# A decoder layer on one core: row maxima from 32-row score chunks, normalisations on ScalarE, softplus steps regrouped, and three of every eight C products on VectorE

## The chip, the cores and the metric

One core of one Trainium2 chip runs the whole program. The metric is the device time of one execution in microseconds, the median of several runs. The kernel before took 5991.21 us (median of 3 runs, 5989.22 to 5993.96).

## The reference

The layer works on x of 64 batches x 128 tokens x 512 features, fp32, with a context of the same shape. Three residual parts follow each other, each on a layer norm of x:

```
x = x + mixer(layernorm(x))              # selective scan
x = x + cross_attention(layernorm(x), ctx)
x = x + experts(layernorm(x))            # top 2 of 8
```

The mixer projects 512 to 2 x 1024 channels (h and gate), runs a causal convolution of 4 taps and silu on h (giving u), projects u to a step size (through 128) and to B and C of 16 states, and takes `dt = softplus(...)`, `dA = exp(dt * A)`, `dBx = dt * u * B`. The state `h[t] = dA[t] * h[t-1] + dBx[t]` runs over the 128 tokens for each of 1024 channels x 16 states; `y = sum over states of h * C + D * u`, times silu(gate), projected back to 512.

The attention treats the 512 features as positions: 8 heads of 16, and each position attends to those at most 64 away (`|q - k| <= 64`), softmax over the keys. The output goes through a projection, relu, a product with ctx and a last projection. The experts part is a router over 8 experts with the top two kept, and experts of width 16.

## The kernel before, in words

The work goes in groups of two batches (GB = 2), 32 groups. One round of the main loop carries three groups at once: group g in the scan of the mixer, group g+1 in the mixer's front (norm, input projections, convolution, B and C, step sizes), group g-1 in the attention, and group g-2 in the experts. Each engine has its own instruction list for a round (the function `iteration` of each engine's block). These lists are written out by hand, step by step; every engine works strictly in its order, and semaphores say when a step may start. The loop body holds two rounds.

The scan is 64 steps s per round: 8 channel blocks ic of 128 (s // 8) x 8 pairs r of states (s % 8), two states and two batches in one tile of 128 x 512. A step passes through all engines:

- ScalarE, `decays` (L479): two exponentials of 128 x 254 into PSUM bank s % 2 (DAR = 2), so it waits for the scan of step s-2.
- GpSimd, `times_b` (L296): du x B into slot s % 8 of the ring (RING = 8), when TensorE has finished with step s-8.
- VectorE, `scan` (L1417): the recurrence, from PSUM and the ring slot, into the ring slot.
- GpSimd or VectorE, `times_c` (L305 or L1402): the slot times C. VectorE does those in `DVE_C`, before: s % 8 = 7.
- TensorE, `y_sum` (L1018, L1025): transposes two steps at a time and sums them over states in PSUM, and frees the slots. The order of y_sum is fixed, a pair waits for both products.

Around it, per round:

- Layer norms, six per round (three uses "a", "t", "e", for mixer, attention and experts, x 2 batches). VectorE takes the statistics and adds epsilon (`norm_stats`, L1363 to L1372), GpSimd takes the power -0.5 (`rstd`, L284), VectorE subtracts the mean and multiplies (`normalise`, L1376, 128 x 512). TensorE then transposes (L896) or projects (L919) the result.
- Softplus, four pairs q of channel blocks: ScalarE makes z, abs, exp(-|z|) in `soft` (two buffers), 1 + exp in `tmp` (L507), ln (L511) in place; VectorE corrects the rounding in `soft_step` 1 to 3 and makes dt x u in step 4 (L1386 to L1397). The ln waits for step 1, since it overwrites `soft`.
- Attention, per batch (i): four blocks of 128 query rows. In the score block `s` (L942) TensorE first writes a mask with `masked` (L906: band values through an identity in bf16, 16 matmuls, the first of them 32x128 and the others 32x32), adds the scores of 8 heads (a 32-row group for each of four heads, keys in a window of 192 or 256), and VectorE takes the negated row maximum (L1464) from all four banks. The next score block waits for this maximum. The maxima are transposed (L952) and added to the queries (L1471) so that a second, transposed set of scores `st` (L906, L969) gives exponentials (L591) without a further subtraction.
- ScalarE's functions lie in table sets; exp, ln and silu are in three, and an ACT_TABLE_LOAD stands where the set changes.
- SP's queue brings the input projection in pieces, x, the context, and after the last use of a C row pair r (step 56 + r) the next round's B and C rows (`spread`, waiting for hcd_done or hcp_done by which engine makes that product).

## Time and profile before

| | |
|---|---|
| median of the runs | 5991.21 us |
| profiled execution | 5965.38 us |
| its span | 5963.5 us |
| busy in the span | GpSimd 5176.7, TensorE 5036.6, VectorE 4912.6, ScalarE 4024.9 us |
| mean granted clock of TensorE | 0.951 of full speed |

Busy time is the union of an engine's instructions; instructions of VectorE and ScalarE overlap a little at their ends. The profile names engines PE (TensorE), DVE (VectorE), ACT (ScalarE), POOL (GpSimd). A round of the loop repeats 32 times with a shorter first and last part, so a stretch of the middle shows the kernel better than the whole span.

### The profile page before, as it was taken

To read this page: it belongs to the slowest core of one execution; us is meant where nothing else is said; L and a number is where in the kernel's file an instruction comes from. 1 tells how busy PE (TensorE), PEld (TensorE's weight loads), DVE (VectorE), ACT (ScalarE), POOL (GpSimd) and SP (SyncE) were. 2 spreads that over 40 slices of the span, in tenths; PEclk is the share of its full clock that TensorE was granted. 3 is DMA by queue.
4 is the path that set the end of the run, shared out by engine and by line. 5 is a ranking of instruction groups with operands and counts; after the bars stand their busy time and mean duration, and the time that the engine had idled before them with its cause. 6 is when DMAs were issued, how large, how long until landed. Compare 5 with 4: busy or idle time off the path is not lost.

```text
span 5963.5 us, 117386 instructions
## 1 busy us (share of the span) xinstructions
PE 5036.6 (84%) x40772; PEld 3515.4 (59%) x40772; DVE 4912.6 (82%) x6563; ACT 4024.9 (67%) x7680; POOL 5176.7 (87%) x4040
## 2 busy tenths in 40 slices
PE   5788888888888888888888888888888888888876
PEld 3556666666565666556566666666656566566643
DVE  3788988888888888988888888888888888888862
ACT  3676776777676777777677666767667677676651
POOL 3998999899999989999899899989999899898870
PEclk8899999999999999999999999999999999999985
DMA  3221211121211221211121111221112121111100
GB/s 103 66 65 31 72 60 65 65 68 35 68 65 60 68 68 35 65 65 63 65 68 55 45 65 64 68 65 49 50 65 67 61 68 48 52 65 63 54 11 6
DMA packets 114455, 348.74 MB, mean 58 GB/s; under 512 B 12912, under 2 KB 14704, under 8 KB 113776
## 3 DMA queue, kind: packets, MB, share of 16 engines
q1 hardware_dynamic: 113904, 341.48, 17.6%
q8 instruction: 336, 5.51, 0.4%
q14 instruction: 215, 1.76, 0.1%
HBM read 323.60 MB, written 17.83 MB: 57 GB/s over the span
## 4 chain that ended last, share of the span: by engine, by line
PE 33%; issue 21%; DVE 19%; ACT 13%; POOL 13%; DVEq 1%; ACTq 0%; POOLq 0%; DMA 0%; SPq 0%
DVE ring L1417 8%; POOL ring L296 7%; PE ps L1073 6%; POOL ring L305 5%; ACT ps L479 5%; PE ps L906 4%; PE ps L1025 4%; PE ps L942 3%; PE ps L969 3%; PE ps L1093 2%; DVE nmax L1464 2%; ACT probs_mem L591 2%; PE ps L1102 2%; PE ps L1108 2%; PE ps L1005 2%
## 5 line engine op out<-in xcount | busy, mean ns | idle before, releaser
L296 POOL TENSOR_TENSOR ring<-du,bc 128x512 f32<-128x512 f32 x2048 | 2747.9, 1355 | 291.4 <-PE ps L1025 182.8
L1417 DVE TENSOR_TENSOR_SCAN ring<-ps,ring 128x512 f32<-128x512 f32 x2048 | 2459.4, 1211 | 455.2 <-ACT ps L479 431.8
L305 POOL TENSOR_TENSOR ring<-ring,bc 128x512 f32<-128x512 f32 x1792 | 2389.4, 1342 | 300.9 <-DVE ring L1417 287.9
L479 ACT ACTIVATE ps<-delta,a_neg 128x254 f32<-128x254 f32 x4096 | 1770.0, 468 | 525.0 <-DVE ring L1417 519.1
L1025 PE MATMUL ps<-ident,ring 128*128 128x128 f32 x8192 | 1127.5, 284 | 83.4 <-POOL ring L305 74.3
L1025 PEld LDWEIGHTS ps<-ident,ring 128*128 128x128 f32 x8192 | 972.0, 146 | 275.1 <-issue 186.4
L906 PE MATMUL ps<-band,ident_bf 32*32 32x512 bf16 (+1 forms) x8192 | 402.5, 406 | 320.8 <-DVE nmax L1464 88.5
L1464 DVE TENSOR_REDUCE nmax<-ps 128x8 f32<-128x1536 f32 (+1 forms) x256 | 516.9, 2019 | 168.0 <-PE ps L942 166.2
L591 ACT ACTIVATE probs_mem<-ps 128x768 f32<-128x768 f32 (+1 forms) x512 | 445.4, 909 | 212.6 <-PE ps L969 208.4
L1073 PE MATMUL ps<-xt_a,w_in 128*128 128x256 f32 x2048 | 483.7, 390 | 55.9 <-ACT gate_t L550 50.0
L1093 PE MATMUL ps<-w_in,xt_a 128*128 128x256 f32 x2048 | 502.7, 401 | 15.5 <-DVE hc L1557 8.1
L1073 PEld LDWEIGHTS ps<-xt_a,w_in 128*128 128x128 f32 x2048 | 384.1, 192 | 158.4 <-ACT gate_t L550 76.3
L1055 PE MATMUL ps<-w_outp,yz 128*128 128x512 f32 x1024 | 469.7, 602 | 0.0
L1093 PEld LDWEIGHTS ps<-w_in,xt_a 128*128 128x128 f32 x2048 | 403.4, 201 | 109.3 <-issue 34.9
L906 PEld LDWEIGHTS ps<-band,ident_bf 32*32 32x32 bf16 (+1 forms) x8192 | 115.9, 89 | 581.7 <-issue 199.6
L1557 DVE SCALAR_TENSOR_TENSOR hc<-ps,conv_w,hc 128x254 f32<-128x254 f32 (+2 forms) x768 | 363.4, 474 | 61.3 <-ACT hc L536 39.5
L980 PE MATMUL ps<-probs_mem,v_aug 128*32 128x192 f32 (+1 forms) x4096 | 239.4, 365 | 102.2 <-ACT probs_mem L591 102.2
L1402 DVE TENSOR_TENSOR ring<-ring,bc 128x512 f32<-128x512 f32 x256 | 312.4, 1220 | 2.3
L1055 PEld LDWEIGHTS ps<-w_outp,yz 128*128 128x128 f32 x1024 | 191.4, 194 | 192.2 <-issue 190.0
L942 PE MATMUL ps<-qk 32*128 32x192 f32 (+1 forms) x4096 | 303.3, 416 | 0.0
L969 PE MATMUL ps<-qk 32*128 32x192 f32 (+1 forms) x4096 | 279.9, 389 | 0.0
L919 PE MATMUL ps<-xb,w_qk 128*128 128x512 f32 x512 | 245.4, 602 | 36.1 <-DVE x_res L1435 35.7
(129 smaller groups left out, 6575.2 us busy)
## 6 DMA issues: line engine op xcount, KB each, us to landing
w_in<-in_w_in SPq DMA_DIRECT2D x256, 512.0 KB, 3.7
bc<-bc_rows SPq DMA_DIRECT2D x256, 512.0 KB, 4.3
x_new<-in_x SPq DMA_DIRECT2D x32, 512.0 KB, 6.9
x_res<-in_x SPq DMA_DIRECT2D x32, 512.0 KB, 6.1
enc<-in_ctx SPq DMA_DIRECT2D x64, 256.0 KB, 4.4
out<-x_att SPq DMA_DIRECT2D x32, 512.0 KB, 2.9
w_outp<-in_w_outp SPq DMA_DIRECT2D x1, 2048.0 KB, 8.1
bc_rows<-bc_sb SPq DMA_DIRECT2D x32, 32.0 KB, 1.5
```

Of the source, the lines that this page charges most:

```text
L296: nc.gpsimd.tensor_tensor(ring[:, s % RING, :].rearrange("p (n t) -> p n t", n=2), du[:, q % 2, (ic % 2) * NT:(ic % 2 + 1) * NT].rearrange ...
L305: nc.gpsimd.tensor_tensor(ring[:, s % RING, :], ring[:, s % RING, :], bc[:, s % RS, 2:4, :].rearrange("p a t -> p (a t)"), ALU.mult).then_ ...
L479: nc.scalar.activation(ps[:, s % DAR, (n % 2) * NT:(n % 2 + 1) * NT].rearrange("p (b t) -> p b t", b=GB)[:, :, 1:T], delta[:, ic, :].rearr ...
L591: nc.scalar.activation(probs[:, :, blk, lo:hi], ps[:, PS_ATT:PS_ATT + 4, (n % 2) * WIN + lo:(n % 2) * WIN + hi], ACT.Exp).then_inc(p_done, 1)
L906: nc.tensor.matmul(ps[rows, PS_ATT + hp, :].rearrange("p (j w) -> p j w", j=2), ident_bf[r:r + 32, cols], band[r:r + 32, a:a + 1, :].to_br ...
L942: last = nc.tensor.matmul(ps[:, PS_ATT + hp, j * WIN + lo:j * WIN + hi], qk[r:r + 32, j, n * P:(n + 1) * P], qk[r:r + 32, 2 + j, at:at + h ...
L1025: last = nc.tensor.matmul(ps[:, PS_Y, b * T:(b + 1) * T], ring[:, t % RING, n * NT + b * T:n * NT + (b + 1) * T], ident[:], start=False, s ...
L1055: last = nc.tensor.matmul(ps[:, PS_ATT + b, :], yz[:, ic, b * T:(b + 1) * T], w_outp[:, ic, :], start=(ic == 0), stop=(ic == NI - 1))
L1073: last = nc.tensor.matmul(ps[:, PS_B, a * NT:(a + 1) * NT], w_in[:, slot, k, a * P:(a + 1) * P], xt_a[:, k, :], start=(k == 0), stop=(k == ...
L1093: last = nc.tensor.matmul(ps[:, PS_B, b * NT:(b + 1) * NT], xt_a[:, k, b * T:(b + 1) * T], w_in[:, slot, k, :], start=(k == 0), stop=(k == ...
L1417: nc.vector.tensor_tensor_scan(ring[:, s % RING, :], ps[:, s % DAR, :], ring[:, s % RING, :], 0.0, ALU.mult, ALU.add).then_inc(h_done, 1)
L1464: nc.vector.tensor_reduce(nmax[:, n].rearrange("p j (a r) -> p a j r", r=32)[:, :, :, DH], ps[:, PS_ATT:PS_ATT + 4, :].rearrange("p a (j w ...
```

## The change

- `DVE_C` becomes s % 8 in (1, 4, 7): VectorE makes 24 of 64 C products of a round, GpSimd 40.
- The layer norms' last step goes to ScalarE as `Identity(scale * x + bias)`. VectorE makes the bias, -mean x rstd, in a new op of one column (`shift`); `rstd` takes both batches in one call for "e" and "a". The step that was on VectorE is gone.
- The scores for the row maxima are made in chunks of 32 query rows: a chunk sees 160 keys (NEAR = 128 + 32) and no more, so a block holds 2 x 160 columns in each bank. The mask of such a chunk is the same for each of the four (`near`, four 32x128 matmuls with a new constant `ident4`, and eight short ones more in the first and last block). The scores are 32 matmuls of 32x32 where 8 of 32x128 were. The row maximum reads 1280 elements a row.
- `masked`, now for the transposed scores alone, has 16 matmuls of 32x32, without the wide first one; a semaphore that nobody waits for is raised ahead of it.
- Softplus: `soft` has one buffer, the ln writes a tile of its own (`lnv`) and waits for the exp alone; abs and exp of the next pair wait for the correction step and the ln of the one before.
- The lists of all four engines are written anew (only the number and kind of steps told above differ).

```diff
+    NEAR = P + 32
-    DVE_C = [s for s in range(64) if s % 8 in (7,)]
+    DVE_C = [s for s in range(64) if s % 8 in (1, 4, 7)]
...
-        soft = sb("soft", [P, 2, 2 * NT])
+        soft = sb("soft", [P, 2 * NT])
+        lnv = sb("lnv", [P, 2 * NT])
...
+        ln_nm = {k: sb("ln_nm_" + k, [P, GB]) for k in "ate"}
...
# GpSimd
-            def rstd(use, g, b):
-                pool.wait_ge(ln_eps[use], g * GB + b + 1)
-                nc.gpsimd.tensor_tensor(ln_rs[use][:, b:b + 1], ln_rs[use][:, b:b + 1], neg_half[:, 0:1],
-                                        ALU.pow).then_inc(ln_rstd[use], 1)
+            def rstd(use, g, b, n=1):
+                pool.wait_ge(ln_eps[use], g * GB + b + n)
+                nc.gpsimd.tensor_tensor(ln_rs[use][:, b:b + n], ln_rs[use][:, b:b + n], neg_half[:, 0:n],
+                                        ALU.pow).then_inc(ln_rstd[use], n)
...
# ScalarE
+            def normalise(use, g, b, dst, src, done):
+                act.wait_ge(ln_shift[use], g * GB + b + 1)
+                nc.scalar.activation(dst, src[:, b, :], ACT.Identity, scale=ln_rs[use][:, b:b + 1],
+                                     bias=ln_nm[use][:, b:b + 1]).then_inc(done, 1)
...
             def soft_exp(g, q):
                 pq = g * NQ + q
-                reached(act, dt_done, pq - 1)
+                reached(act, sp_c, pq)
+                reached(act, sp_ln, pq)
...
             def soft_ln(g, q):
-                act.wait_ge(sp_c, g * NQ + q + 1)
-                nc.scalar.activation(soft[:, q % 2, :], soft[:, q % 2, :], ACT.Ln, bias=1.0).then_inc(sp_ln, 1)
+                pq = g * NQ + q
+                act.wait_ge(sp_exp, pq + 1)
+                reached(act, dt_done, pq)
+                nc.scalar.activation(lnv[:], soft[:], ACT.Ln, bias=1.0).then_inc(sp_ln, 1)
...
# TensorE
+            def near(n):
+                for hp in range(4):
+                    r = 32 * hp
+                    nc.tensor.matmul(ps[:, PS_ATT + hp, 0:NJ * NEAR].rearrange("p (j w) -> p j w", j=NJ),
+                                     ident4[r:r + 32, :], band[r:r + 32, 0:1, 0:NEAR].to_broadcast([32, NJ, NEAR]),
+                                     start=True, stop=False, skip_group_check=True)
+                for a, lo, hi in {0: ((0, 0, 64), (1, 0, 32)), NBLK - 1: ((2, P, NEAR), (3, P - 32, NEAR))}.get(n, ()):
+                    for hp in range(4):
+                        r = 32 * hp
+                        nc.tensor.matmul(ps[32 * a:32 * a + 32, PS_ATT + hp, 0:NJ * NEAR].rearrange("p (j w) -> p j w", j=NJ)[:, :, lo:hi],
+                                         ident_bf[r:r + 32, r:r + 32], band[r:r + 32, 3:4, 0:hi - lo].to_broadcast([32, NJ, hi - lo]),
+                                         start=False, stop=False, skip_group_check=True)
...
             def masked():
                 for a in range(4):
                     for hp in range(4):
                         r = 32 * hp
-                        wide = a == 0 and hp == 0
-                        rows, cols = (slice(0, P), slice(0, P)) if wide else (slice(32 * a, 32 * a + 32), slice(r, r + 32))
-                        nc.tensor.matmul(ps[rows, PS_ATT + hp, :].rearrange("p (j w) -> p j w", j=2),
-                                         ident_bf[r:r + 32, cols], band[r:r + 32, a:a + 1, :].to_broadcast([32, 2, WIN]),
-                                         start=(a == 0 or hp > 0), stop=False, skip_group_check=True)
+                        nc.tensor.matmul(ps[32 * a:32 * a + 32, PS_ATT + hp, :].rearrange("p (j w) -> p j w", j=2),
+                                         ident_bf[r:r + 32, r:r + 32], band[r:r + 32, a:a + 1, :].to_broadcast([32, 2, WIN]),
+                                         start=True, stop=False, skip_group_check=True)
...
-                    masked()
+                    near(n)
                     for j in range(NJ):
-                        for hp in range(4):
-                            r = 32 * hp
-                            last = nc.tensor.matmul(
-                                ps[:, PS_ATT + hp, j * WIN + lo:j * WIN + hi],
-                                qk[r:r + 32, j, n * P:(n + 1) * P], qk[r:r + 32, 2 + j, at:at + hi - lo],
-                                start=False, stop=True, skip_group_check=True)
+                        for a in range(4):
+                            k0 = n * P + 32 * a - 64
+                            lo, hi = max(0, -k0), min(NEAR, H - k0)
+                            for hp in range(4):
+                                r = 32 * hp
+                                last = nc.tensor.matmul(
+                                    ps[32 * a:32 * a + 32, PS_ATT + hp, j * NEAR + lo:j * NEAR + hi],
+                                    qk[r:r + 32, j, n * P + 32 * a:n * P + 32 * a + 32], qk[r:r + 32, 2 + j, k0 + lo:k0 + hi],
+                                    start=False, stop=True, skip_group_check=True)
...
# VectorE
-            def normalise(use, g, b, dst, src, done):
+            def shift(use, g, b):
                 dve.wait_ge(ln_rstd[use], g * GB + b + 1)
-                nc.vector.tensor_scalar(dst, src[:, b, :], ln_mv[use][:, b, 0:1], ln_rs[use][:, b:b + 1],
-                                        ALU.subtract, ALU.mult).then_inc(done, 1)
+                nc.vector.tensor_scalar(ln_nm[use][:, b:b + 1], ln_mv[use][:, b, 0:1], ln_rs[use][:, b:b + 1], -1.0,
+                                        ALU.mult, ALU.mult).then_inc(ln_shift[use], 1)
...
                     nc.vector.tensor_reduce(
                         nmax[:, n].rearrange("p j (a r) -> p a j r", r=32)[:, :, :, DH],
-                        ps[:, PS_ATT:PS_ATT + 4, :].rearrange("p a (j w) -> p a j w", j=NJ)[:, :, :, lo:hi],
+                        ps[:, PS_ATT:PS_ATT + 4, 0:NJ * NEAR].rearrange("p a (j w) -> p a j w", j=NJ),
                         AX.X, ALU.max, negate=True).then_inc(max_done, 1)
```

In the new order, the two silus of u follow each other in two places: beside gate silu and an ln at step 39, beside the other gate silu at step 48. In the attention of the second batch, each exp has decays on either side.

## Rows read from the trace of the kernel before

**Rows 1.** The profile's page: its head, and each engine's busy time.

```profile
span 5963.5 us, 117386 instructions
...
PE 5036.6 (84%) x40772; PEld 3515.4 (59%) x40772; DVE 4912.6 (82%) x6563; ACT 4024.9 (67%) x7680; POOL 5176.7 (87%) x4040
```

**Rows 2.** One ScalarE copy, in all and between 200 and 500 us: count, durations, starts.

```profile
L565 ACT COPY bc_sb<-ps x32: 361/361/362, 84.4 to 5590.7; 32x256 f32<-32x256 f32 x32
...
L565 ACT COPY bc_sb<-ps x2: 361/362/362, 237.7 to 410.2; 32x256 f32<-32x256 f32 x2
```

**Rows 3.** Busy time of each engine in a stretch of ten rounds.

```profile
2014.30:3800.70 1786.40, 1549.06 (x12817) 1086.52 (x12810) 1542.98 (x2061) 1267.16 (x2423) 1626.40 (x1268) 0.97 0.19 60
```

**Rows 4.** Waits in these ten rounds: total us, times, longest.

```profile
ACT ps L479 <- DVE ring L1417: 154.8, 120, 3.9
DVE ring L1417 <- ACT ps L479: 131.1, 90, 4.0
POOL ring L305 <- DVE ring L1417: 83.9, 69, 2.9
POOL ring L296 <- PE ps L1025: 61.1, 41, 4.0
...
DVE nmax L1464 <- PE ps L942: 44.1, 44, 1.9
...
DVE yg L1411 <- PE ps L1025: 23.5, 31, 1.3
```

**Rows 5.** Groups of VectorE and GpSimd in the ten rounds: busy us, mean ns | idle before.

```profile
L1402 DVE TENSOR_TENSOR ring<-ring,bc 128x512 f32<-128x512 f32 x81 | 96.7, 1193 | 0.7
L1464 DVE TENSOR_REDUCE nmax<-ps 128x8 f32<-128x2048 f32 x40 | 91.2, 2281 | 18.6 <-PE ps L942 18.1
L1464 DVE TENSOR_REDUCE nmax<-ps 128x8 f32<-128x1536 f32 x40 | 70.4, 1759 | 26.3 <-PE ps L942 26.0
...
L1376 DVE TENSOR_SCALAR probs_mem<-x_att,ln_mv_e,ln_rs_e 128x512 f32<-128x512 f32 x20 | 24.3, 1215 | 0.0
L1376 DVE TENSOR_SCALAR xb<-x_res,ln_mv_t,ln_rs_t 128x512 f32<-128x512 f32 x20 | 21.5, 1075 | 4.4 <-POOL ln_rs_t L284 4.4
L1376 DVE TENSOR_SCALAR x_new<-x_new,ln_mv_a,ln_rs_a 128x512 f32<-128x512 f32 x20 | 20.2, 1008 | 0.0
...
L1372 DVE TENSOR_SCALAR ln_rs_a<-ln_mv_a 128x1 f32<-128x1 f32 x20 | 3.1, 154 | 0.7
...
L296 POOL TENSOR_TENSOR ring<-du,bc 128x512 f32<-128x512 f32 x645 | 865.8, 1356 | 71.8 <-PE ps L1025 61.1 <-DVE du L1397 10.2
L305 POOL TENSOR_TENSOR ring<-ring,bc 128x512 f32<-128x512 f32 x562 | 748.5, 1341 | 88.2 <-DVE ring L1417 83.9
...
L284 POOL TENSOR_TENSOR ln_rs_a<-ln_rs_a,neg_half 128x1 f32<-128x1 f32 x20 | 11.9, 596 | 0.0
```

**Rows 6.** C products over the span (shortest/median/longest ns), and one in the timeline.

```profile
L1402 DVE TENSOR_TENSOR ring<-ring,bc x256: 658/1298/1761, 121.3 to 5785.5; 128x512 f32<-128x512 f32 x128
...
L305 POOL TENSOR_TENSOR ring<-ring,bc x1792: 1252/1271/1796, 103.6 to 5784.0; 128x512 f32<-128x512 f32 x200
...
3013.47 1.53 DVE L1402 TENSOR_TENSOR ring<-ring,bc 128x512 f32<-128x512 f32 x1
3014.93 1.21 DVE L1417 TENSOR_TENSOR_SCAN ring<-ps,ring 128x512 f32<-128x512 f32 x1
```

**Rows 7.** Groups of ScalarE in the ten rounds: busy us, mean ns | idle before.

```profile
L479 ACT ACT_TABLE_LOAD x60 | 77.0, 1283 | 1.1
L578 ACT ACTIVATE qk<-ps,b_qk 128x512 f32<-128x512 f32 x80 | 52.2, 677 | 12.9 <-PE ps L919 12.9
```

**Rows 8.** Timeline of one score block on TensorE: start us, length us, instructions.

```profile
3035.73 0.73 PE L906 MATMUL ps<-band,ident_bf 32*128 32x512 bf16 x16 [2.36 <-ACT v_aug L582]
3036.39 0.93 PE L942 MATMUL ps<-qk 32*128 32x192 f32 x16
...
3036.03 0.14 PEld L906 LDWEIGHTS ps<-band,ident_bf 32*32 32x32 bf16 x15 [0.24 <-issue]
```

More of the change, by code:

```diff
@@ new lines, in iteration @@
+                if p1:
+                    attention(g, p2, 1, "exp", 1)
+                if cur:
+                    decays(g, 46)
+                if nxt:
+                    tap3(j, 3)
+                if p1:
+                    attention(g, p2, 1, "exp", 2)
+                if cur:
+                    decays(g, 47)
+                if p1:
+                    attention(g, p2, 1, "exp", 3)
+                if cur:
+                    skip_term(g, 7)
+                    decays(g, 48)
+                if nxt:
+                    u_silu(j, 2)
+                    u_silu(j, 3)
```

751 lines of the change are left out of this document (370 added, 381 removed).

## The prediction

> **What bounds the kernel now.** I read the page's busy line first: GpSimd, TensorE, VectorE and ScalarE are all busy for 67 to 87% of the span [rows 1]. One share of the whole says little here, so I then asked for the length of a round. The same ScalarE copy comes once in each round, from its third appearance at 410.2 to its 32nd at 5590.7 us: 5180.5 / 29 = 178.6 us [rows 2]. A stretch of exactly ten rounds gives, for one round, GpSimd 162.6, TensorE 154.9, VectorE 154.3 and ScalarE 126.7 us of work [rows 3]. So nothing is full: even GpSimd is idle for 16.0 us and VectorE for 24.3.
>
> The view of waits over the same ten rounds says why [rows 4]. VectorE's scans wait 13.1 us a round for ScalarE's decays, and the decays wait 15.5 for the scans: they share two banks, so each can be two steps ahead at most. 4.4 us go to score blocks from TensorE and 2.4 to y sums. GpSimd waits 8.4 for scans and 6.1 for ring slots that TensorE frees. Nobody waits long for GpSimd: its name is missing as a releaser of VectorE in front of the scans. It is the fullest engine, but its ring is eight deep. The reader is to see a net of four engines that is 9% longer than its fullest member, whose tightest link is scan against decay.
>
> **The change by parts, for one round.**
> VectorE gains 16 more C products. One takes 1193 ns [rows 5]; its shortest is 658 and its median 1298 [rows 6], so about half is waiting for something. An op that follows without a wait starts some 0.08 us before the end of the one ahead (in the timeline, a product of 1.53 us at 3013.47, the next scan at 3014.93) [rows 6], so I charge 16 x 1.11 = +17.8 us. Six normalisations of 1215, 1075 and 1008 ns leave, two of each [rows 5]: 6 x 1.02 net = -6.1. Six shifts of one column come, at the 154 ns of the neighbouring one-column op: +0.5 net. The row maxima: 2281 ns for 2048 elements and 1759 for 1536 give 1.02 ns an element and 0.19 us fixed; 1280 elements are then 1.50 us, against a mean of 2.02: 8 x 0.52 = -4.2. VectorE: 154.3 + 17.8 - 6.1 + 0.5 - 4.2 = 162.3 us.
>
> GpSimd loses 16 products. Undisturbed one takes 1.25 to 1.27, the mean is 1.34 to 1.36 [rows 5, 6]. The excess of (1.356 - 1.26) x 64 + (1.341 - 1.26) x 56 = 10.7 us a round belongs to the some 30 VectorE ops a round that read two tiles of SBUF or normalise (8 products, 16 softplus steps, 6 normalisations): 0.36 us each. There will be 40, so +3.6. Two rstd calls fewer, 0.6 us each [rows 5]: -1.2. 162.6 - 16 x 1.26 + 3.6 - 1.2 = 144.8 us. From the spread of 658 to 1761 ns [rows 6], product against product, I read a turn-taking: each waits for the other for about half an instruction. The Trainium skill (SBUF — State Buffer, the definition of the shared port pair) says more: an exclusive lock held for the whole instruction, the loser fully blocks. That speaks against this change, which raises the number of such ops; by it every product on VectorE, meeting a GpSimd that is 91% busy, would wait 0.91 x 1.26 / 2 = 0.57 us, an estimate. By that rule, the trace agrees (1193 - 658 = 535 ns). The measured wait is inside the 1.11 that I charge, and it should fall a little as GpSimd's share falls from 91 to 82%.
>
> ScalarE takes six normalisations with a scale and a bias column: the like op of 512 columns from PSUM takes 677 ns [rows 7], 6 x 0.60 net = +3.6. Its table loads, counted as changes among exp, ln and silu along the written orders, fall from 14 a round to 12, since the silus of u come in pairs beside a gate silu: -2 x 1.283 = -2.6 [rows 7]. ScalarE: 127.7 us.
>
> TensorE. The mask in front of scores was one wide 32x128 matmul and 15 small ones: 0.73 us, and scores of 192 columns 0.93 in 16 passes [rows 8]. The 15 small ones wait about 0.30 us behind the wide one (3035.73 to 3036.03), then start together: 15 loads within 0.14 us. In the transposed scores the wide one goes, 8 x 0.30 = -2.4. In the row-maxima scores the mask is four matmuls of 320 columns (and eight short ones in two blocks of four), the scores 64 passes of 160 columns in place of 16. If 16 small tiles run side by side as in the mask, that is again four turns: 0.93 x 160 / 192 = 0.78, plus 0.3 to 0.4 for the mask, against 0.66 + 0.86 to 1.15 before: about -0.4. Bound below -0.6; bound above, column tiles in series, 16 turns of 0.93 / 4 = 3.7 us: +2.4. I take -0.4 since the mask row is the same tile form: 8 x -0.4 = -3.2. TensorE: 154.9 - 2.4 - 3.2 = 149.3. The Trainium skill (TensorE: Matmul & The Clock Gate, "The mechanism") has weight loads overlap matmuls in flight only where the row group differs. By it the four column tiles of a row group would go one after another, and the sum would carry the upper bound; the trace does not agree for bf16 (15 loads of all four row groups in 0.14 us), fp32 is not shown here.
>
> The rest is order and buffers. The ln no longer waits for a VectorE step, and the softplus of the next round starts some two to three steps earlier; I cost that at nothing, since no view has it as a large wait in the ten rounds. On SP's queue the reloads of bc behind steps 57 and 60 now wait for VectorE's products instead of GpSimd's; they stand at most one scan behind their own and hide as before. If that cover went, the first B products of a round would stand, on GpSimd, which has slack now.
>
> **From work to time.** VectorE now is the fullest, 162.3 where GpSimd had 162.6; all others have less. What matters is how much VectorE idles. I went along both written orders in stretches of four scans, priced every step with the mean of its row, and compared VectorE with ScalarE (before, this gives 151.9 and 127.5 a round, near the measured 154.3 and 126.7 [rows 3]). ScalarE's excess over VectorE, summed over stretches in which it is the longer, is 12.4 us before, close to the 13.1 measured [rows 4]; in the new order it is 5.2, because the exps stand apart and the products fill VectorE's gaps. The other 11.2 us of idle (24.3 - 13.1) are score blocks, y sums, and small waits; with lighter TensorE and GpSimd, and VectorE arriving later, I take 9.5. Sum: 162.3 + 5.2 + 9.5 = 177.0, and 0.5 less for shorter waits at the shared reads: 176.5, -2.1 us a round. Over 31 rounds -65 us, and -5 in the last two rounds, where the chain of scores and maxima is bare. The profiled execution had 5965.4 us (span 5963.5) and its kernel's median is 5991.2, 26 us more; the same step from the median gives 5991 - 70 = 5921, say 5920. No change can be told below 0.2%, 12 us or 0.4 us a round.
>
> **Rivals.**
> *VectorE becomes the bound and keeps its idle.* Its work is +8.0 us; if idle does not shrink from 24.3, a round is 186.6 and the time 5991 + 8.0 x 31 = 6239. It decides from 16.3 us of idle on. For it: the link to ScalarE is two deep, tighter than the ring that GpSimd had; by loads alone two products of eight would have balanced the engines (VectorE 162.3 - 8 x 1.11 = 153.4, GpSimd 144.8 + 8 x 0.9 = 152.0). Against it: ScalarE caused over half of that idle, and more VectorE work between scans is what hides it. Halfway, 20.3 us idle, gives 5991 + 4.0 x 31 = 6115; most of this rival's mass lies between there and no change. Chance 0.31, 0.03 of it beyond 6115.
> *Small fp32 tiles run in series.* TensorE +19 us a round in the row-maxima blocks instead of -3.2, work 171.7; its idle of 23.7 would have to fall to 6.9 to break even, and each of the eight blocks hands VectorE 2.4 us more to wait. With half of that passed on, +10 us a round, 6300. Chance 0.06, low because the mask's small tiles did run together [rows 8]. This is what the rule of the Trainium skill cited above (TensorE: Matmul & The Clock Gate, "The mechanism") would make of the new block.
> *The work freed on GpSimd was what paced the round.* Then a round follows the sum of stretch maxima with all three engines: VectorE, ScalarE and GpSimd (10.2 before, 9.0 after, in four steps), 175.3 before and 172.3 after; with cheaper shared reads and idle under 11 us it reaches 172, -6.6 x 31 = -205: 5786. For it: GpSimd is 91% busy; against: few wait for it. Chance 0.15.
> *Nothing moves*, gains and losses cancel within 12 us: 0.08, 5991.
> Forecast, 5850 to 5975: 0.40.
>
> **Numbers.** Faster is the forecast and the GpSimd rival, 0.55; same 0.08; slower 0.37. Range 5790 to 6115: it leaves out the tail of the GpSimd rival (0.05), of the VectorE rival (0.03) and the serial tiles (0.06).
>
> **What would show it.** A round of 176 to 177 us; VectorE 161 to 163 of work in it and its scans waiting 5 to 7 us for ScalarE in place of 13; C products on VectorE at 1.1 to 1.2 us, maxima at 1.50; GpSimd 143 to 146; 12 table loads; a score block of 64 passes in about 0.8 us. I am wrong if the scans' wait for decays is still over 10 us, if y sums wait on VectorE's late products (some stand four scans behind), or if score blocks take over 2 us.

## The result, and the profile after

The changed kernel takes 5532.0 us (median of 4 runs, 5530.5 to 5538.8) against 5990.2 for the kernel before, run beside it: a ratio of 0.9239 (95% interval 0.9223 to 0.9255), 458 us less. The forecast had the sign and 70 us. Its profiled execution has a span of 5531.6 us. The page's head and busy line, as in [rows 1], and its four costliest groups (busy us, mean ns | idle before and its releaser):

```profile
span 5531.6 us, 139169 instructions
...
PE 4796.2 (87%) x51012; PEld 3435.7 (62%) x51012; DVE 4955.4 (90%) x7075; ACT 4058.8 (73%) x7812; POOL 4541.5 (82%) x3464
...
L300 POOL TENSOR_TENSOR ring<-du,bc 128x512 f32<-128x512 f32 x2048 | 2741.9, 1356 | 577.7 <-PE ps L1066 352.3
L1454 DVE TENSOR_TENSOR_SCAN ring<-ps,ring 128x512 f32<-128x512 f32 x2048 | 2456.7, 1211 | 201.2 <-POOL ring L300 103.1
L309 POOL TENSOR_TENSOR ring<-ring,bc 128x512 f32<-128x512 f32 x1280 | 1776.5, 1394 | 232.5 <-DVE ring L1454 230.6
L1439 DVE TENSOR_TENSOR ring<-ring,bc 128x512 f32<-128x512 f32 x768 | 755.4, 987 | 3.4
```

VectorE has 768 products where it had 256, yet its busy time over the span is only 43 us more [rows 1]. The copy of [rows 2], in all and in its second and third appearance, and the window of ten rounds as in [rows 3]:

```profile
L566 ACT COPY bc_sb<-ps x32: 362/362/362, 86.0 to 5185.7; 32x256 f32<-32x256 f32 x32
...
L566 ACT COPY bc_sb<-ps x2: 362/362/362, 220.1 to 381.0; 32x256 f32<-32x256 f32 x2
...
2038.90:3695.90 1657.00, 1478.30 (x15941) 1062.53 (x15942) 1542.86 (x2211) 1265.68 (x2441) 1417.05 (x1081) 0.98 0.20 65
```

A round is (5185.7 - 381.0) / 29 = 165.7 us, 12.9 less than before. VectorE works 154.3 us in it, as it did before, and is idle for 11.4 in place of 24.3. (The window before holds 645 scans where ten rounds have 640. Cut from first scan to first scan, over rounds 3 to 30, the round is 178.1 before and 165.4 after, with 153.4 and 154.2 of work.) So the gain of a round stands in VectorE's idle time, and its added work has all but vanished: two things to explain. 31 x 12.9 = 400 us; the first and the last rounds give 32 of the span's 431.9, and most of the 26 that are left is the distance of the profiled execution before from its median (25). Waits and groups of these ten rounds, as in [rows 4] (us, times, longest) and [rows 5, 7]:

```profile
DVE ring L1454 <- ACT ps L462: 29.9, 29, 1.9
DVE ring L1454 <- POOL ring L300: 29.3, 39, 1.3
DVE nmax L1489 <- PE ps L982: 18.0, 30, 1.1
DVE yg L1448 <- PE ps L1066: 5.6, 10, 0.6
POOL ring L300 <- PE ps L1066: 119.1, 76, 4.3
...
L1439 DVE TENSOR_TENSOR ring<-ring,bc 128x512 f32<-128x512 f32 x241 | 232.4, 968 | 1.0
L1489 DVE TENSOR_REDUCE nmax<-ps 128x8 f32<-128x1280 f32 x80 | 119.0, 1487 | 19.5 <-PE ps L982 18.0
L1430 DVE TENSOR_TENSOR delta<-delta,lnv 128x512 f32<-128x512 f32 x40 | 27.3, 682 | 0.0
L1563 DVE TENSOR_TENSOR small<-iota,small 128x16 f32<-128x16 f32 x20 | 2.6, 172 | 0.3
L469 ACT ACTIVATE x_new<-x_new,ln_nm_a,ln_rs_a 128x512 f32<-128x512 f32 x20 | 16.2, 812 | 0.0
```

VectorE's three large waits have shrunk: for decays 13.1 to 3.0 us a round, for score blocks 4.4 to 1.8, for y sums 2.4 to 0.6. A new one came, for GpSimd's B products, 2.9. GpSimd now waits 11.9 a round for slots. And one product costs 968 ns, not 1193.

### The profile page after: what moved, and what is told of

Same layout as the page of the kernel before. It is cut to its first block, busy times and chain, and to the rows that moved or that the text cites. A ratio compares the mean times of both kernels' runs of the same rounds, so it can differ in the third digit from the quotient of the medians.

```text
span 5531.6 us, 139169 instructions
## 1 busy us (share of the span) xinstructions
PE 4796.2 (87%) x51012; PEld 3435.7 (62%) x51012; DVE 4955.4 (90%) x7075; ACT 4058.8 (73%) x7812; POOL 4541.5 (82%) x3464
## 4 chain that ended last, share of the span: by engine, by line
PE 46%; DVE 18%; issue 15%; POOL 11%; ACT 7%; DVEq 1%; POOLq 0%; ACTq 0%
POOL ring L300 7%; PE ps L1066 7%; PE ps L1114 6%; DVE ring L1454 5%; PE ps L1096 5%; PE ps L982 4%; PE ps L957 4%; POOL ring L309 4%; PE ps L1134 3%; PE ps L1010 3%; DVE nmax L1489 3%; ACT ps L462 3%; DVE ring L1439 2%; DVE tmp L1423 2%; PE ps L1021 1%
## 5 line engine op out<-in xcount | busy, mean ns | idle before, releaser
L309 POOL TENSOR_TENSOR ring<-ring,bc 128x512 f32<-128x512 f32 x1280 | 1776.5, 1394 | 232.5 <-DVE ring L1454 230.6
L1066 PE MATMUL ps<-ident,ring 128*128 128x128 f32 x8192 | 1103.7, 282 | 73.7 <-DVE ring L1439 43.1
L1439 DVE TENSOR_TENSOR ring<-ring,bc 128x512 f32<-128x512 f32 x768 | 755.4, 987 | 3.4
L592 ACT ACTIVATE probs_mem<-ps 128x768 f32<-128x768 f32 (+1 forms) x512 | 455.9, 911 | 176.0 <-PE ps L1010 174.4
L1134 PE MATMUL ps<-w_in,xt_a 128*128 128x256 f32 x2048 | 488.8, 394 | 12.8 <-DVE hc L1582 8.1
L1489 DVE TENSOR_REDUCE nmax<-ps 128x8 f32<-128x1280 f32 x256 | 380.7, 1487 | 78.4 <-PE ps L982 73.8
L982 PE MATMUL ps<-qk 32*32 32x160 f32 (+2 forms) x16384 | 296.2, 297 | 0.0
L1010 PE MATMUL ps<-qk 32*128 32x192 f32 (+1 forms) x4096 | 286.8, 397 | 0.0
L579 ACT ACTIVATE qk<-ps,b_qk 128x512 f32<-128x512 f32 x256 | 170.6, 678 | 125.6 <-PE ps L957 125.6
L1010 PEld LDWEIGHTS ps<-qk 32*128 32x128 f32 x4096 | 186.3, 197 | 68.4 <-issue 63.1
```

What stands on the lines that cost most here:

```text
L309: nc.gpsimd.tensor_tensor(ring[:, s % RING, :], ring[:, s % RING, :], bc[:, s % RS, 2:4, :].rearrange("p a t -> p (a t)"), ALU.mult).then_ ...
L982: last = nc.tensor.matmul(ps[32 * a:32 * a + 32, PS_ATT + hp, j * NEAR + lo:j * NEAR + hi], qk[r:r + 32, j, n * P + 32 * a:n * P + 32 * a ...
L1010: last = nc.tensor.matmul(ps[:, PS_ATT + hp, a * WIN + lo:a * WIN + hi], qk[r:r + 32, 2 + j, blk * P:(blk + 1) * P], qk[r:r + 32, j, at:at ...
L1066: last = nc.tensor.matmul(ps[:, PS_Y, b * T:(b + 1) * T], ring[:, t % RING, n * NT + b * T:n * NT + (b + 1) * T], ident[:], start=False, s ...
L1134: last = nc.tensor.matmul(ps[:, PS_B, b * NT:(b + 1) * NT], xt_a[:, k, b * T:(b + 1) * T], w_in[:, slot, k, :], start=(k == 0), stop=(k == ...
L1439: nc.vector.tensor_tensor(ring[:, s % RING, :], ring[:, s % RING, :], bc[:, s % RS, 2:4, :].rearrange("p a t -> p (a t)"), ALU.mult).then_ ...
```

## The experiments

What the recorded expectations call the theories: **A**, the gain lies in which engine does what (A1: GpSimd paced the round before; A2: VectorE's work paces the round after). **B**, it lies in the new order alone. **C**, work and order are each worth little apart. Later **D**: the new order lives on a GpSimd with slack. **E**: the kernel after with C products back on GpSimd is slow only because no order was made for that. **F**: in the old order the scans' link to ScalarE's decays is the pace.

All medians in us, ratios to the kernel before with their 95% intervals; the other columns are us of one round (a window of ten, divided by ten); idle is the round less VectorE's busy time. Rounds are those of the one profiled execution; before, it was 0.4% faster than its median.

| run | median | ratio (interval) | round | VectorE busy, idle | GpSimd |
|---|---|---|---|---|---|
| before | 5990 | 1 | 178.6 | 154.3, 24.3 | 162.6 |
| after | 5532 | 0.924 (0.922-0.926) | 165.7 | 154.3, 11.4 | 141.7 |
| order_only | 6169 | 1.030 (1.027-1.033) | 186.0 | 160.2, 25.8 | 158.2 |
| parts_only | 6075 | 1.016 (1.015-1.018) | 182.9 | 155.9, 27.0 | 144.8 |
| b_scores_new | 5871 | 0.982 (0.980-0.983) | 175.9 | 150.3, 25.6 | 161.0 |
| b_c3 | 6107 | 1.021 (1.020-1.023) | 182.4 | 164.3, 18.1 | 145.4 |
| b_norm_act | 6146 | 1.026 (1.023-1.029) | 184.5 | 149.4, 35.1 | 160.8 |
| b_pool_light | 5973 | 0.998 (0.997-1.000) | 179.3 | 153.4, 25.9 | 143.6 |
| b_no_tables | 5956 | 0.996 (0.994-0.997) | 179.1 | 154.9, 24.2 | 162.6 |
| a_c1 | 5851 | 0.982 (0.976-0.988) | 175.0 | 150.5, 24.5 | 159.4 |
| a_c2 | 5604 | 0.936 (0.933-0.939) | 168.0 | 151.2, 16.8 | 151.7 |
| a_norm_dve | 5791 | 0.969 (0.967-0.970) | 174.4 | 162.0, 12.4 | 143.2 |
| a_scores_old | 5809 | 0.972 (0.970-0.974) | 173.6 | 158.5, 15.1 | 141.6 |
| a_soft_old | 5679 | 0.950 (0.946-0.953) | 170.0 | 153.6, 16.4 | 142.3 |
| a_exp_bunch | 5532 | 0.925 (0.922-0.929) | 165.5 | 155.0, 10.6 | 141.9 |
| a_late1 | 5896 | 0.984 (0.981-0.987) | 177.7 | 160.6, 17.1 | 144.6 |
| a_moved3 | 5584 | 0.933 (0.931-0.934) | 167.2 | 153.7, 13.5 | 141.6 |
| a_pool_heavy | 5992 | 1.001 (0.999-1.003) | 180.4 | 165.1, 15.3 | 163.8 |

### Order and work taken apart

**order_only**: the kernel after (its lists, its softplus) with the work of before: 8 C products on VectorE, normalisations there, old score blocks and masks.

```diff
-    DVE_C = [s for s in range(64) if s % 8 in (1, 4, 7)]
+    DVE_C = [s for s in range(64) if s % 8 in (7,)]
-                    shift("e", g - 2, 0)
+                    experts_norm(g - 2, 0)
-                    near(n)
+                    masked()
```

> The new orders of all engines and the new softplus buffers, but with the work of before: one C product of eight on VectorE, normalisations on VectorE, score blocks and masks of before. Theory A, the gain lies in which engine does what (GpSimd relieved, the locked reads rarer, VectorE's maxima cheaper): the work per round is that of before, so 5850 to 6050 us. Theory B, the gain lies in the order alone (scans no longer wait for decays): 5530 to 5700 us, with the scans' wait for decays under 5 us a round against 13.

**a_c1**: the kernel after with that first line of the diff alone, the 16 products in GpSimd's list.

> The kernel after with one C product of eight on VectorE instead of three; GpSimd has the other sixteen, at their numerical place in its list. Theory A1, GpSimd paced the round before and the sixteen products are the main gain: 5800 to 5950 us, GpSimd busy over 90% in the middle. Theory B (order) or one of the other parts: 5530 to 5650 us. VectorE's work falls by 16 x 0.9 = 14 us a round, so if VectorE bounded the kernel after, it would even be faster than 5532.

**b_c3**: the kernel before with the opposite line; VectorE makes the added products one scan behind their own.

> The kernel before with three C products of eight on VectorE, each put one scan behind its own; all else as before. Theory A1 (GpSimd paced the round): 5700 to 5850 us. Theory B: the products fall into an order not made for them and add 16 x 1.1 = 18 us of VectorE work: 6000 to 6300 us.

**b_scores_new**: the kernel before with the new score block of 32-row chunks and the maximum over 1280 elements.

> The kernel before with the new score blocks (chunks of 32 rows, 1280 elements a maximum), the transposed scores' mask as before. VectorE's work falls by 4.2 us a round and a score block by some 0.4 us. If VectorE's work or the chain of score block and maximum paced the round: 5850 to 5900 us. If neither: 5960 to 5990 us, within 0.5% of before.

Neither half pays. The order alone costs 3.0%, the products alone 2.1% in the old order, and the score block, the only part that helps there, gives 1.8%. The window of order_only, its waits in it, and its products:

```profile
2091.10:3951.20 1860.10, 1572.51 (x12725) 1097.13 (x12726) 1602.31 (x2049) 1230.21 (x2376) 1582.07 (x1238) 0.95 0.18 58
...
DVE nmax L1468 <- PE ps L950: 78.7, 70, 3.7
DVE ring L1432 <- ACT ps L478: 72.2, 70, 2.3
DVE ring L1432 <- POOL ring L300: 57.2, 30, 2.5
...
L1417 DVE TENSOR_TENSOR ring<-ring,bc 128x512 f32<-128x512 f32 x80 | 137.2, 1715 | 1.4
```

The new order halves the wait for decays (7.2 us a round in place of 13.1 [rows 4]), and pays for it with score blocks (7.9), B products (5.7) and products of 1715 ns on average. That mean hides one place: in 8 of the ten rounds the product of step 31 took 7.7 us, and the other 72 products took 1051 ns. One of the eight on VectorE, then GpSimd beside it:

```profile
3138.07 7.70 DVE L1417 TENSOR_TENSOR ring<-ring,bc 128x512 f32<-128x512 f32 x1
...
3137.81 7.42 POOL L300 TENSOR_TENSOR ring<-du,bc 128x512 f32<-128x512 f32 x6
3147.10 1.27 POOL L300 TENSOR_TENSOR ring<-du,bc 128x512 f32<-128x512 f32 x1 [1.87 <-PE ps L1034]
```

Six B products of GpSimd went by back to back, and VectorE's product ended 0.55 us after the last of them, when GpSimd had to wait for a slot. I call this a long lockout: an instruction that waited for more than one of GpSimd's (over 1.85 us). Of 27 rounds in the middle of this trace, first scan to first scan, the 20 with a long lockout last 187.9 us and the 7 without 180.0, against 178.1 in the kernel before. So most of what the order alone costs is this one place; without it, it would be some 1%, an estimate from these rounds of one execution.

**parts_only**: the counterpart, all of the new work in the old lists and with the old softplus (b_c3, b_scores_new and the old-order move of the norms below, together).

> The reverse of the first run: the orders and softplus buffers of before, with the work of after: three C products of eight on VectorE one scan behind, new score blocks and masks, normalisations on ScalarE. VectorE's work is that of before (+10.0 -4.0 -5.4 us a round by the runs so far), GpSimd's 17 us less. Theory A (work alone): 5532 to 5650 us. Theory C (work and order are worth little apart, since the order has to open the places for the products): 5800 to 5950 us.

6075 us. So the two by two is 5990, order +3.0%, work +1.6%, both -7.6%: theory C, and more than it asks, since the two halves are losses, that of the order mostly by the long lockout at step 31. Window and first wait:

```profile
2064.60:3893.40 1828.80, 1520.22 (x15979) 1088.87 (x15970) 1559.26 (x2211) 1307.99 (x2467) 1447.69 (x1103) 0.96 0.18 59
...
DVE ring L1450 <- ACT ps L466: 170.7, 101, 5.1
```

Here every engine has about the load of the kernel after (VectorE 155.9, GpSimd 144.8), and the round is 17.2 us longer. Equal loads, other idle time: 17.1 us a round of waiting for decays. That fits F for the old order; b_no_tables below limits it.

### Each part taken out of the new kernel

**a_norm_dve**: the normalisations back on VectorE, in the places of the shifts.

```diff
-                    shift("t", g - 1, 0)
+                    attention_x(g - 1, 0)
```

> The kernel after with the normalisations back on VectorE, where their shifts stood; ScalarE's are gone. VectorE's work rises by 6 x (1.1 - 0.2) = 5.4 us a round. If VectorE's work paces the round after (theory A2): 5532 + 31 x 5.4 = 5700 us or more. If ScalarE is the one that paces it, it is relieved of 4.8 us and the time stays within 5480 to 5560 us.

**a_scores_old**: old score blocks and masks in the new order.

> The kernel after with the score blocks and masks of before. VectorE's work rises by 4.3 us and TensorE's by 7 us a round. Theory A2: VectorE alone gives 5532 + 31 x 4.3 = 5665 us; if the chain of score block and maximum counts too, more than that, 5700 to 5800 us. If neither paces the round, under 5580 us.

**a_soft_old**: the old softplus buffers and waits; for this, VectorE's first step of pair 3 had to go two scans ahead of where it stood.

```diff
-                nc.scalar.activation(lnv[:], soft[:], ACT.Ln, bias=1.0).then_inc(sp_ln, 1)
+                act.wait_ge(sp_c, g * NQ + q + 1)
+                nc.scalar.activation(soft[:, q % 2, :], soft[:, q % 2, :], ACT.Ln, bias=1.0).then_inc(sp_ln, 1)
```

> The kernel after with the softplus buffers and waits of before (two soft buffers, ln in place behind VectorE's first step); one VectorE step had to move two scans ahead for it. Work and table loads are the same. If the new buffers matter: 5560 to 5650 us; my expectation is no more than 0.5% from 5532.

**a_c2**: s % 8 in (4, 7), so 16 products on VectorE and 48 on GpSimd.

> The kernel after with two C products of eight on VectorE (steps 4 and 7), GpSimd has those of step 1 again. By work alone this is the best balance (VectorE 154 - 7, GpSimd 142 + 10). If VectorE's work plus a fixed idle of 11 us sets the round: 5450 us. If GpSimd's slack is what keeps the idle and the waits at the shared reads small: between 5532 and 5851, 5600 to 5750 us.

Against the 5532 of the kernel after, going without the part costs 319 us (all of the moved products, a_c1), 72 (half of them, a_c2), 259 (norms), 277 (scores) and 147 (softplus). Without the 72, which lie within the 319, that sums to 1002 for a gain of 458. The parts can't be added up; each one that was also tried in the old kernel is worth more beside the others (products -124 and +319 us, scores 113 and 277, norms -159 and +259). The norms are the clearest: they cost 2.6% in the old order (b_norm_act, below) and are worth 4.5% in the new. The first eight products moved to VectorE (a_c1 to a_c2) save 7.0 us a round, the second eight 2.3: most of it lies between 56 and 48 products on GpSimd. Long lockouts are a part of both: a_c1 has them in 21 of the 27 middle rounds (175.8 us with, 170.2 without), a_c2 in 7 (170.7 with, 165.6 without), the kernel after in none (165.4). In a round without one, the second eight products are worth no more than 0.2 us; by these rounds their gain is that no long lockout is left.

Theory A2 is borne out in part. a_norm_dve gives VectorE 7.7 us more work and the round is 8.7 longer; a_scores_old gives it 4.2 more and TensorE 5.3, and the round is 7.9 longer (5809, just above the range that I gave); but a_c2 takes 3.1 us off VectorE and the round is 2.3 longer, so its work alone does not set the round.

The softplus edit, which I had costed at nothing, and again at no more than 0.5% before this run, is seen in a_soft_old, on ScalarE and then on the scans:

```profile
ACT soft L509 <- DVE tmp L1420: 91.3, 20, 7.7
...
DVE ring L1451 <- ACT ps L461: 75.0, 60, 3.1
```

ScalarE stands 9.1 us a round for VectorE's first softplus step, decays stand behind it, and the scans' wait for them goes from 3.0 to 7.5. Since one step was moved too, I can't say how much of the 147 us is the buffers'.

### Is it the decays, or GpSimd?

**b_pool_light**: the kernel before, GpSimd's C products of steps 1 and 4 of 8 on two columns only. Those products are left out of the result.

```diff
+                w = 2 if s % RS in (1, 4) else 2 * NT
```

> The kernel before, in which GpSimd's C products of steps 1 and 4 of every eight work on 2 columns in place of 512, so its work falls by some 17 to 20 us a round and nobody takes it over. It leaves out that part of the products. Theory A1 (a full GpSimd paces the round before): 5450 to 5700 us. If it has to be VectorE's or ScalarE's time that falls: 5900 to 5990 us.

**b_norm_act**: the kernel before with the normalisations on ScalarE, between decays.

> The kernel before with the normalisations on ScalarE, set between decays where VectorE's stood. VectorE's work falls by some 5.5 us a round. If in the old order a round is VectorE's work plus 24 to 27 us of idle, as in the five runs with it: 5983 - 31 x 5.5 = 5810 us or, with the idle at 27, 5890 us. If the longer way of a normalisation through two engines counts: 5950 us or more.

**b_no_tables**: the kernel before with silu and ln replaced by the identity, so that no table is loaded; softplus, silu and what hangs on them are not computed.

> The kernel before, in which ScalarE's silu and ln are replaced by identity, so that no table loads are left but the first: 14 x 1.28 = 18 us a round off ScalarE, no other engine's work changes. It computes something else in those places. Theory F, in the order of before the link of scans to ScalarE's decays paces the round (13 us of VectorE's idle): most of it goes, 5550 to 5750 us. If it behaves like the GpSimd relief of the same size (5973): ScalarE is not the pace either, and VectorE's idle has no single owner.

**a_pool_heavy**: the kernel after, and 16 products that nobody needs on GpSimd, into a spare tile, in the places of the 16 that left.

```diff
+            def extra(g, s, k):
+                reached(pool, spare_done, g * 16 + k)
+                nc.gpsimd.tensor_tensor(spare[:], w_outp[:, 0, :], w_outp[:, 1, :], ALU.mult).then_inc(spare_done, 1)
```

> The kernel after plus sixteen products of GpSimd per round that nobody needs (two resident weight tiles multiplied into a spare tile of bf16), at the places where the sixteen products would be if GpSimd still made them. Nothing else changes: VectorE still has its 24. Theory D, the new order lives on a GpSimd with slack: GpSimd's work returns to 160 us a round and the time to 5750 us or more, as in the run with one product of eight (5851), whose round was 9.4 us longer though VectorE had 4 us less to do. Theory E, that run was slow only since its order was not made for it: under 5600 us.

b_pool_light and a_pool_heavy settle A1 and D. Windows of b_pool_light, b_norm_act and a_pool_heavy, a wait of the second, groups and a wait of the third:

```profile
2195.70:3988.30 1792.60, 1552.05 (x12756) 1087.21 (x12749) 1533.97 (x2050) 1257.33 (x2402) 1435.89 (x1261) 0.97 0.18 60
```
```profile
2081.00:3926.00 1845.00, 1581.63 (x12768) 1105.79 (x12761) 1494.45 (x2051) 1303.80 (x2465) 1608.17 (x1261) 0.95 0.18 58
...
DVE ring L1448 <- ACT ps L480: 209.6, 100, 5.1
```
```profile
2023.00:3827.00 1804.00, 1528.54 (x15932) 1079.19 (x15933) 1651.19 (x2210) 1274.91 (x2439) 1637.61 (x1239) 0.96 0.18 60
...
L1462 DVE TENSOR_TENSOR ring<-ring,bc 128x512 f32<-128x512 f32 x240 | 255.8, 1069 | 1.0
L1453 DVE TENSOR_TENSOR delta<-delta,lnv 128x512 f32<-128x512 f32 x40 | 42.8, 1069 | 0.0
L1586 DVE TENSOR_TENSOR small<-iota,small 128x16 f32<-128x16 f32 x20 | 13.5, 711 | 0.3
...
DVE ring L1477 <- POOL ring L303: 61.0, 36, 2.6
```

In the old order GpSimd can be relieved of 19.0 us a round and nothing happens (-0.2%, at the edge of what can be told). In the new order the same load put back takes all of the gain away, though every other instruction and its place in its list are those of the kernel after. A1 falls, D stands. And the window says where it went: of 14.7 us more a round, VectorE's idle takes 3.9 (3.2 of it scans that wait for GpSimd's B products, 6.1 against 2.9) and its *busy time* 10.8 (154.3 to 165.1). No work was added there; its instructions got longer. Both engines are then over 90% busy, so this tells where the time lies, not which of the two engines leads. The softplus addition went from 682 to 1069 ns, even a router step of 16 columns from 172 to 711.

b_norm_act takes 4.9 us of work off VectorE and makes the round 5.9 longer: the scans wait 21.0 us a round for decays. With parts_only this suggests that an instruction of ScalarE between two decays is dear in the old lists; it isn't shown apart from the longer way through two engines. Taking 19 us off ScalarE (b_no_tables) gives only 0.5%, where F as I had put it asked for 5550 to 5750 us, so its load isn't the pace. F holds as "the wait shows here", not as "the load sets it".

### Places

**a_exp_bunch**: the kernel after with every second exp of the attention directly behind its partner, without decays between (my reason for the smaller wait).

> The kernel after with every second exp of the attention directly behind its partner on ScalarE, where the new order has decays between them. Work is the same. If the spreading of ScalarE's long steps is what removed the scans' wait for decays (3 us in place of 13 a round), this brings some 3 to 6 us a round back: 5630 to 5720 us. If not: within 0.5% of 5532.

**a_late1**: in the kernel after, VectorE's 24 products stand directly behind their own scan (7 of them), one scan behind it (6), two (6), three (1) or four (3), and the last in the next round. Here the 23 all stand one scan behind, so that 17 move.

```diff
-                    scan(g, 17)
-                    times_c(g, 17)
+                    scan(g, 17)
...
+                    scan(g, 18)
+                    times_c(g, 17)
```

> The kernel after with each of VectorE's 24 products put one scan behind its own, where it stood in the run that had the old orders and the new parts. If that run was slow because of this placing, this one is slow too: 5650 us or more. If the rest of the new order carries the gain: 5520 to 5580 us. The products' mean duration, set by what GpSimd does when they start, may move from 0.97 us to 0.88 to 0.93, its value in the two runs with this placing.

**a_moved3**: three of the four longest products (steps 1, 49, 57, about 1.7 us in every round; step 23, which takes 1.76 as well, I had overlooked, and it stayed) moved by one or two instructions, to where GpSimd's instruction would be nearly over.

> The kernel after with three of VectorE's 24 products moved by one or two instructions: step 1 behind y_step 7, step 49 beside the product of step 52, step 57 behind the normalised attention output. In the kernel after these three take 1.62, 1.76 and 1.77 us in nearly every round, where the others take 0.66 to 1.3. If the waits at the shared reads are the cost and the rest holds: up to 3 x 1.0 us a round less VectorE work, 5440 to 5530 us. If the phase of the whole round shifts and other products run into GpSimd's instead: 5540 to 5650 us.

a_exp_bunch: 5532.05, the very median of the kernel after. Exps standing apart are worth nothing; my reason was a story. a_late1: +364 us against the kernel after, for moving 17 products by one to three scans. Its window:

```profile
2170.40:3947.00 1776.60, 1513.72 (x15966) 1081.09 (x15970) 1605.70 (x2211) 1271.16 (x2444) 1446.01 (x1082) 0.96 0.19 61
```

6.3 us of the 12.0 a round is busy time again (the products themselves 24 x 0.086 = 2.1, the rest other instructions that wait longer or no longer stand back to back), 5.7 idle. The products' mean rose to 1054 ns, where I had expected 880 to 930. a_moved3 did shorten the products' mean (968 to 927 ns: step 1 from 1.62 to 1.35 us, step 57 from 1.77 to 1.08, while step 49 stayed at 1.76), but y sums came later, and the round grew by 1.5 us; its wait, 5.6 us in the kernel after:

```profile
DVE yg L1448 <- PE ps L1066: 16.6, 20, 1.2
```

So a product's place is a bargain between the meeting with GpSimd and the slot that TensorE waits for.

### What a meeting with GpSimd costs

From the profiled executions, in ten rounds, VectorE's products and softplus steps and, in before and order_only, its six normalisations, by number a round, their time, and what of it is over the shortest of their kind (0.66 us each, 0.52 for a normalisation):

```
kernel         number  us     waiting  mean product
before         30      31.3   12.2     1193
after          40      37.8   11.4      968
order_only     30      36.3   17.3     1715
parts_only     40      39.4   13.0      930
a_pool_heavy   40      43.8   17.4     1069
a_late1        40      41.2   14.8     1054
```

A third more such instructions, and less waiting in all. (Products and softplus steps alone are 24 before and 40 after, with 8.8 and 11.4 us of waiting, so 0.37 and 0.29 us each.) In the timeline of the kernel after, VectorE then GpSimd (start us, length us):

```profile
2037.31 1.22 DVE L1454 TENSOR_TENSOR_SCAN ring<-ps,ring 128x512 f32<-128x512 f32 x1 [0.94 <-ACT ps L462]
2038.45 1.75 DVE L1439 TENSOR_TENSOR ring<-ring,bc 128x512 f32<-128x512 f32 x1
2040.12 1.21 DVE L1454 TENSOR_TENSOR_SCAN ring<-ps,ring 128x512 f32<-128x512 f32 x1
2041.26 0.66 DVE L1439 TENSOR_TENSOR ring<-ring,bc 128x512 f32<-128x512 f32 x1
...
2037.13 1.30 POOL L309 TENSOR_TENSOR ring<-ring,bc 128x512 f32<-128x512 f32 x1
2038.36 2.97 POOL L300 TENSOR_TENSOR ring<-du,bc 128x512 f32<-128x512 f32 x2
2041.29 1.75 POOL L309 TENSOR_TENSOR ring<-ring,bc 128x512 f32<-128x512 f32 x1
```

The first product starts 0.09 us after a GpSimd instruction and takes 1.75 us: the 1.21 that GpSimd's has left, and 0.54 more. In the kernel before too, a product's time is what is left plus 0.55 us (0.98 left gives 1.53, 0.53 gives 1.08), and never under 0.66. The second starts just before GpSimd's next, takes 0.66, and GpSimd's takes 1.75 in place of 1.27. In the kernel before, products that start 200 to 400 ns into a GpSimd instruction take 1555 ns on average, at 600 to 800 ns 1070, at 1000 to 1200 ns 694. It is full exclusion, and in these rows whoever starts first wins. The Trainium skill (SBUF — State Buffer, the shared port pair) calls it an exclusive lock whose loser fully blocks; by that rule, the trace agrees, with 1.75 = 1.21 left + 0.54.

The long lockouts show that starting first isn't always enough, and that the loser can lose more than once. From a_c1, VectorE then GpSimd:

```profile
2857.24 6.76 DVE L1455 TENSOR_TENSOR ring<-ring,bc 128x512 f32<-128x512 f32 x1
...
2857.29 1.27 POOL L300 TENSOR_TENSOR ring<-du,bc 128x512 f32<-128x512 f32 x1
2858.52 1.27 POOL L309 TENSOR_TENSOR ring<-ring,bc 128x512 f32<-128x512 f32 x1
2859.74 3.71 POOL L300 TENSOR_TENSOR ring<-du,bc 128x512 f32<-128x512 f32 x3
```

The product's record starts 0.05 us ahead of GpSimd's instruction, yet five of GpSimd's pass at 1.27 us each, back to back, before it runs. Of over 2.6 us, whole traces have 24 such lockouts of products in order_only (7.6 to 9.5 us), 27 in a_c1 (4.9 to 8.8), 8 in a_c2 (5.5 to 7.9), and of a softplus step 30 in b_scores_new (4.2 to 4.4), 7 in b_norm_act (3.5 to 4.0) and 4 in the kernel before (3.9). Three other runs have one or two; the kernel after has none. What decides between one lost turn and five isn't shown.

The point for an order written by hand is that a given place mostly has the same duration in every round: in ten rounds of the kernel after, 18 of 24 places stay within 35 ns (some always 0.66 to 0.69, steps 23, 49 and 57 always 1.75 to 1.78), and only steps 39 and 41 vary by 0.5 us or more. The wait isn't an average that falls on every product, it belongs to places.

## Why the prediction was right in sign and wrong in size

Predicted: a round of 176.5, VectorE 162.3 of work and 14.2 of idle. Measured: 165.7, of 154.3 and 11.4. Of the 10.8 us missed a round, 8.0 are work and only 2.8 idle. In time, 31 x 10.8 = 335 of the 388 us missed; the rest lies in the first and last rounds (32 gained, 5 forecast) and in the profiled execution before, which was faster than its median.

- **The step that failed is the charge of 16 x 1.11 us for the moved products.** It took the mean of eight products that met a 91% busy GpSimd, and called the wait a property of the instruction ("it should fall a little"). Measured: 24 x 0.968 - 8 x 1.193 = +13.7, less the 1.3 of overlap that I counted, so 12.4 where I had 17.8: 5.4 of the 8.0. The rest are small terms: neighbouring instructions overlap by 12.7 us a round against 10.6 before, 2.1 more and not 1.3; softplus and router steps got shorter by some 0.9 us in all; and the window of [rows 3] held five scans too many, 0.8 us. a_pool_heavy is the test: with GpSimd as full as before, VectorE's work is 165.1, near my 162.3, though not by the same sum: its products average 1069 ns, so load gives back 101 of the 225 ns that the mean had lost, and small steps take the rest. The other 124 ns are left for the places, which fits a_late1: with GpSimd's load near that of the kernel after, its mean is 1054. I had moved the load and the places and priced the product as if neither had moved.
- **The idle time**: 14.2 forecast, 11.4 measured; decays 3.0 (I had 5.2), the rest 8.4 (9.0). The size was near by luck, since its reason, the exps that stand apart, is worth nothing (a_exp_bunch). The comparison of written orders by stretches of four scans found a true property of the order, but order_only, which has the same lists, is slower than before. The comparison left out GpSimd and TensorE, and so the lockouts.
- **Softplus at nothing** was wrong: undoing it, together with one moved step, costs 147 us.
- **The sizes that held**: row maximum 1487 ns (1.50); GpSimd 141.7 us (144.8); TensorE 147.8 (149.3); ScalarE 126.6 (127.7), where the new normalisation takes 0.81 us and not 0.68; table loads 12 a round. The shift takes 0.19 us, not 0.154.
- **Rival of small fp32 tiles in series**: refuted. TensorE's timeline of one block of 64 passes:

```profile
3095.46 0.32 PE L928 MATMUL ps<-band,ident 32*128 32x320 bf16 x4
3095.71 0.23 PE L935 MATMUL ps<-band,ident_bf 32*32 32x128 bf16 x8
3095.76 1.17 PE L982 MATMUL ps<-qk 32*32 32x128 f32 x64
3096.86 0.66 PE L921 MATMUL ps<-ident,x_new 128*128 128x128 f32 x4
...
3095.73 0.87 PEld L982 LDWEIGHTS ps<-qk 32*32 32x32 f32 x64
```

  From the mask's start to the next matmul it is 1.40 us, against 3.7 for the scores alone in series; 64 weight loads go by in 0.87 us beside matmuls in flight. The passes took 1.17 where I had 0.78, the mask as forecast. The overlap rule of the Trainium skill (TensorE: Matmul & The Clock Gate, "The mechanism"), which, as the prediction read it, would have made this block three times as long, isn't what this trace shows.
- **Rival of VectorE as the bound**: VectorE did become the fullest engine (154.3 of 165.7, 93%), but its idle halved. What a fuller VectorE does in the old order is b_c3: 10.0 us more work, 6.2 less idle, a round 3.8 longer.
- **Rival of GpSimd as the pace** (5786, chance 0.15): for the wrong reason the nearest. Freeing GpSimd alone gives nothing (b_pool_light), so it did not pace the round. In the new order a full GpSimd takes the whole gain back (a_pool_heavy), 10.8 of 14.7 us a round through VectorE's own durations. The range's lower end, 5790, came from this rival, and no term of mine reached 5532.

Three things stay open. Which engine's list carries the effect of the order wasn't tried. The part of VectorE's idle in the old order that remains under a light GpSimd (25.9 us) wasn't traced further than to the decays. And TensorE's granted clock moves with the runs: of a round, 9.2 us were at the lower level of 1.2 GHz before, 6.8 after, but 19.1 in order_only, 18.4 in b_norm_act and 15.7 in a_pool_heavy. In order_only TensorE is busy for 29% of a long lockout, and 6.8 us at the lower level stand at its end. No run holds the clock fixed, so its share isn't shown apart; if each us at the lower level made half a us of TensorE's work, an estimate, it would be 1.2 of the 12.9 us between before and after, and up to 5 of order_only's loss.

## What to carry to other kernels

Where engines run fixed lists, judge neither a shift of load nor an order alone: order and work lost 3.0% and 1.6% here by themselves and gained 7.6% together, so a trial of one part in a list that was made for other loads says little about it. A single place can make such a trial lose: look at the longest duration of a group, not only at its mean. When you price an instruction whose mean holds waiting, ask what the other engine does at the new place and with the new load, and price it at its undisturbed time plus that meeting. An engine that nobody is seen waiting for can still cost time, in the busy time of its neighbour: the views of waits don't show it, the spread of one group's durations does.

## What the runs showed that I had not expected

- A busier GpSimd makes VectorE's instructions on SBUF longer down to the smallest: 128x16 steps of the router from 172 to 711 ns, a copy of 128x256 with one input from 0.29 to 1.30 us, when GpSimd's work rose from 141.7 to 163.8 us a round (a_pool_heavy).
- One meeting is paid once: of two products next to each other (steps 49 and 52 in a_moved3) the first took 1.76 and the second 0.68 us.
- One product can stay locked out for 7.7 us while six instructions of GpSimd go by at full speed; in order_only the rounds in which this happens are 7.9 us longer than the others.
- 64 fp32 matmuls of 32x32 with 128 to 160 columns take 1.17 us together.
- Moving 17 of VectorE's instructions by one to three scans, with no work added, costs 6.6% (5896 against 5532), four fifths of what the whole change gave.
